# GpSimd's long operations and two VectorE steps put elsewhere in slots 3 to 13 of an attention and Fourier-layer kernel

## What is computed

```python
n1 = layernorm(x)
q, k, v = n1 @ wq + bq, ctx @ wk + bk, ctx @ wv + bv
s = (q @ k.T) / sqrt(32) * mask
s = where(s == 0, -1e9, s)
x = x + (softmax(s) @ v) @ wo + bo
n2 = layernorm(x)
out = x + real(ifft(fft(n2) @ (w_real + i * w_imag))) + bias
```

## Time and profile before

| what | value |
|---|---|
| median of 3 runs | 449.24 us (449.22 to 450.0) |
| the profiled execution | 449.74 us, its span 448.0 us |
| PE busy | 431.6 us, 96% of the span |
| DVE busy | 402.7 us, 90% |
| ACT busy | 368.2 us, 82% |
| POOL busy | 361.0 us, 81% |

### The profile page before, as it was taken

The page is one execution under the profiler, slowest core; times in us unless marked ns, Lnnn a source line. Parts: engine busy times, 40 slices in busy tenths (PEclk is TensorE's granted clock), DMA queues, the critical chain, the costliest instruction groups (busy, mean ns, idle before and its releaser), DMA issues.

```text
span 448.0 us, 10895 instructions
## 1 busy us (share of the span) xinstructions
PE 431.6 (96%) x3496; PEld 298.1 (67%) x3496; DVE 402.7 (90%) x532; ACT 368.2 (82%) x1342; POOL 361.0 (81%) x482
## 2 busy tenths in 40 slices
PE   7989999998899999999999999999999999989997
PEld 6877678786576666666776667666666765555444
DVE  3799899899999999999999999999999899999353
ACT  1648989799889989898989998989999899999620
POOL 5769997995779898989989898989898778755763
PEclk9999999999999999999999999999999999999999
DMA  8999754404434454545456554555442324431243
GB/s 271 397 385 221 249 190 113 129 1 119 113 105 93 136 126 119 148 117 139 128 139 137 129 145 113 121 104 130 137 95 64 97 75 96 78 83 35 61 115 121
DMA packets 85286, 60.15 MB, mean 134 GB/s; under 512 B 40141, under 2 KB 72813, under 8 KB 84718
## 3 DMA queue, kind: packets, MB, share of 16 engines
q1 hardware_dynamic: 84508, 59.29, 49.0%
q10 hardware_dynamic: 722, 0.17, 0.2%
HBM read 29.33 MB, written 8.39 MB: 84 GB/s over the span
## 4 chain that ended last, share of the span: by engine, by line
PE 68%; DVE 14%; issue 6%; ACT 5%; POOL 5%; DMA 1%; DVEq 0%; SPq 0%; POOLq 0%; ACTq 0%
PE bank L464 27%; PE bank L469 18%; PE bank L623 8%; PE bank L637 5%; DVE zs L924 4%; PE scores L609 4%; ACT zs L726 3%; DVE zs L917 3%; PE bank L570 2%; POOL cl L1164 2%; PE bank L551 1%; DVE nmin L929 1%; DMA cxs<-in_ctx 1%; PE scores L469 1%; DVE x L902 1%
## 5 line engine op out<-in xcount | busy, mean ns | idle before, releaser
L726 ACT ACTIVATE zs<-zs,nbias 128x128 f32<-128x128 f32 x512 | 199.5, 395 | 18.0 <-POOL nbias L1151 17.3
L726 ACT ACTIVATION_READ_ACCUMULATOR zs<-zs,nbias 128x1 f32 x512 | 98.4, 192 | 0.0
L924 DVE SCALAR_TENSOR_TENSOR zs<-zs 128x1024 f32<-128x1024 f32 x64 | 92.1, 1439 | 1.1
L929 DVE TENSOR_REDUCE nmin<-zs 128x8 f32<-128x1024 f32 x64 | 78.1, 1220 | 2.1
L917 DVE TENSOR_TENSOR zs<-scores,ms 128x1024 f32<-128x1024 f32 x64 | 78.0, 1219 | 0.1
L735 ACT COPY pt<-bank 128x512 f32<-128x512 f32 x128 | 67.8, 580 | 7.4 <-PE bank L623 7.3
L623 PE MATMUL bank<-ident,zs 128*128 128x128 f32 x512 | 67.0, 274 | 1.9 <-ACT zs L726 1.9
L1111 POOL TENSOR_TENSOR xs<-xs,bob 128x512 f32<-128x512 f32 (+1 forms) x41 | 42.8, 1048 | 24.7 <-DVE zs L924 21.6
L623 PEld LDWEIGHTS bank<-ident,zs 128*128 128x128 f32 x512 | 57.5, 140 | 5.6 <-ACT zs L726 4.5
L469 PE MATMUL bank<-xth,wqh 128*128 128x256 f16 x224 | 61.2, 273 | 0.0
L469 PE MATMUL bank<-xth,wql 128*128 128x256 f16 x224 | 61.1, 273 | 0.0
(11 more groups left out here) (125 smaller groups left out, 910.8 us busy)
## 6 DMA issues: line engine op xcount, KB each, us to landing
xs<-in_x SPq DMA_DIRECT2D x16, 512.0 KB, 4.7
xtr<-in_xt SPq DMA_DIRECT2D x16, 512.0 KB, 4.4
out<-x SPq DMA_DIRECT2D x31, 256.0 KB, 2.5
qs<-qh SPq DMA_DIRECT2D x120, 64.0 KB
lp<-in_lparts SPq DMA_DIRECT2D x4, 1024.0 KB, 9.9
qs<-ql SPq DMA_DIRECT2D x60, 64.0 KB
ms<-in_mask SPq DMA_DIRECT2D x16, 128.0 KB, 2.4
wks<-in_wk SPq DMA_DIRECT2D x2, 512.0 KB, 6.8
```

The lines of the kernel that those rows point to most:

```text
L726: last = act.activation(z, z, ACT.Exp, bias=nbias[:, s % 4, i:i + 1], scale=-NEG, accum_out=zsum[:, s % 4, i:i + 1])
L924: dve.scalar_tensor_tensor(out=z, in0=z, scalar=0.0, in1=z, op0=ALU.is_equal, op1=ALU.subtract).then_inc(eq_done, 1)
L929: dve.tensor_reduce(nmin[:, s % 4, :], zs[:, s % NZ].rearrange("p t h k -> p (t h) k"), AX.X, ALU.min).then_inc(mn_done, 1)
```

## The change

Nothing is computed differently, and the same DMAs are issued. Steps move to other places in the lists:

- POOL waits for the zero test of the slot (`eq_done`) from slot 4 on instead of slot 9 on. The long operations of slots 4 to 7 are put behind this wait: fold 6 (was in slot 3) before the bias of slot 4, folds 7 to 9 behind it; fold 10 before and fold 11 behind the bias of slot 5.
- `split_lo` of block 3 moves from slot 3 to slot 6, that of block 4 one slot later, from 6 to 7; each is cut into two halves, one before and one behind the slot's bias. `scale_mask(2)` moves from slot 4 to slot 6.
- `add_bo` of block 2 moves from slot 9 to slot 10; `add_bf(0, 0)` goes behind `scale_mask` in slot 12.
- DVE takes the moments of block 6 in slot 8 (were in slots 10 and 11) and puts them and the moments of the first output rows ahead of M(0)'s rows.
- SP loads `xtr` of block 5 behind the query copies of slot 5 instead of ahead of them.

```diff
--- before.py
+++ after.py
@@ -18,7 +18,6 @@
 NC = NB * S // CH
 NS = 4 * NC
 V0, V1 = 2, NS + 16
-VS = 9
 VP = 4
 VQ = 13
 LAST = ("FF", NC - 1, 1)
@@ -102,7 +101,7 @@
 
 
 def stats_slot(c, t):
-    return 4 if c == 4 else 4 * (c - 4) + 2 + t
+    return 4 if c == 4 else 8 if c == 6 else 4 * (c - 4) + 2 + t
 
 
 def small_slot(c):
@@ -113,13 +112,9 @@
     return 5 if c == 4 else 4 * (c - 3)
 
 
-def lo_slot(c):
-    return 3 if c == 3 else 6
-
-
 def bo_slot(c):
 
-    return c + 7 if c < 3 else 4 * c + 3 if c < 13 else 2 * c + 27
+    return c + 7 if c < 2 else 10 if c == 2 else 4 * c + 3 if c < 13 else 2 * c + 27
 
 
 def build(nc, x, xt, ctx_in, mask, wq, bq, wk, bk, wv, bv, wo, bo, lparts, tables, bf, eye, sums, pick, places, heads, out):
@@ -438,7 +433,9 @@
                     load_mask(c + 2)
                 if r == 0 and 0 <= c - 4 < NC:
                     store(c - 4, 1)
-                if r == 0 and 5 <= c + 4 < NC:
+                if v == 6:
+                    load_xt(5)
+                if r == 0 and 6 <= c + 4 < NC:
                     load_xt(c + 4)
                 if r == 3 and 0 <= c - 2 < NC - 1:
                     turn_x1n(c - 2, 0)
@@ -1054,7 +1051,7 @@
                 if 0 <= v - 9 < 4:
                     low_m(v - 9)
                 for n in mids:
-                    if fills[n][0] == "M":
+                    if fills[n][0] == "M" and v > 8:
                         lo(n)
                 tasks = []
                 tasks += [(stats1, mean1, a, t) for a in range(4, NC) for t in range(2) if stats_slot(a, t) == v]
@@ -1068,6 +1065,8 @@
                     recip((v - 3) // 2)
                 for _, mean, *ct in tasks:
                     mean(*ct)
+                if v == 8:
+                    lo(at["M", 0])
                 if c - 2 == NC - 1 and r < 2:
                     last_lo2(r)
                 if v == 2:
@@ -1230,8 +1229,6 @@
                 c, r = divmod(v, 4)
                 if v == 8:
                     constant_row()
-                if v == VP:
-                    fold(7)
                 for a in range(5, NC):
                     if small_slot(a) == v:
                         stat_cols(a)
@@ -1239,8 +1236,16 @@
                     rstd2(c - 2, 0)
                 if r == 2 and 0 <= c - 2 < NC:
                     rstd2(c - 2, 1)
-                if VS <= v < NS:
+                if VP <= v < NS:
                     pool.wait_ge(eq_done, v + 1)
+                if v == 4:
+                    fold(6)
+                if v == 5:
+                    fold(10)
+                if v == 6:
+                    split_lo(3, slice(0, 2), False)
+                if v == 7:
+                    split_lo(4, slice(0, 2), False)
                 for a in range(5, NC):
                     if v == 4 * a - 11:
                         split_lo(a, slice(0, 2), False)
@@ -1253,15 +1258,19 @@
                         add_bo(a, 1)
                 if 0 <= v < NS:
                     bias(v)
-                for n in {2: (4, 5), 4: (8, 9), 5: (10, 11)}.get(v, ()):
+                for n in {2: (4, 5), 4: (7, 8, 9), 5: (11,)}.get(v, ()):
                     fold(n)
+                if v == 6:
+                    split_lo(3, slice(2, 4))
+                if v == 7:
+                    split_lo(4, slice(2, 4))
                 if v % 2 == 1 and 0 <= v - 5 < NS:
                     ctx_lo((v - 5) // 2)
                 if r == 2 and 0 <= c - 2 < NC - 1:
                     norm_lo2(c - 2, 0)
                 if r == 3 and 0 <= c - 2 < NC - 1:
                     norm_lo2(c - 2, 1)
-                if r < 2 and 0 <= c - 3 < NC:
+                if r < 2 and 0 <= c - 3 < NC and v > 12:
                     add_bf(c - 3, r)
                 if v == 3:
                     low_o(0)
@@ -1279,15 +1288,14 @@
                         add_bo(a, 1, slice(0, D // 2), False)
                     if bo_slot(a) + 3 == v:
                         add_bo(a, 1, slice(D // 2, D))
-                for a in (3, 4):
-                    if lo_slot(a) == v:
-                        split_lo(a)
-                if v == 3:
-                    fold(6)
                 if v > VP and v % 2 == 1 and 0 <= v - 3 < NS:
                     spread((v - 3) // 2)
-                if r == 0 and 2 <= c + 1 < NC:
+                if v == 6:
+                    scale_mask(2)
+                if r == 0 and 3 <= c + 1 < NC:
                     scale_mask(c + 1)
+                if v == 12:
+                    add_bf(0, 0)
 
 
 def frequencies():
```

## The result

The changed kernel takes 456.6 us (median of 4 runs) against 449.36 us for the kernel before, measured again beside it: a ratio of 1.0167, 95% interval 1.015 to 1.0183, 7.2 us slower. The profiled execution took 456.56 us with a span of 454.8. The forecast was 455.4 us, range 451.7 to 457.8.

A forecast was written before the change was run, and what follows sets the result against it. PE was taken as the bound, its earlier losses paid in full at the end. Terms -4.3 + 7.3 + 0.6 + 2.6 = +6.2 us took the profiled 449.74 to 455.9, or 455.4 us against the 449.24 median; range 451.7 to 457.8.

The forecast's parts named there:

- `split_lo` of block 3, +7.3 us: PE idles before QQ(3, 0) from 62.8 us until `xtl` is complete at 70.1 us: +7.3 us, bounds 6.5 and 8.3.
- the stretch of the zero test of slot 6 by `rzb`: Within the block 3 term: zero test of slot 6 meets POOL's `rzb`, takes 1.6 us and ends at 67.5 us.
- +0.3 us: Zero test of slot 6, waiting for all of `rzb`, would end some 0.3 us later; sum 0.3 us higher, not adopted.
- `split_lo` of block 4, +0.6 us: PE waits before QQ(4, 0) for POOL's second half in slot 7: +0.6 us, 0 to 1.5.
- The clock, +2.6 us: PE's clock falls in the idle before QQ(3, 0), so matmuls after it run slowly: +2.6 us, between 0 and 2.6.
- The rival in which it stays up: Same stall before QQ(3, 0), but no slow matmuls after it: 452.8 us, chance 0.25.
- The waits that go, -4.3 us: PE's waits from 28 to 120 us, outside slot 1, all go: -4.3 us, -4.8 to -1.3.
- both long waits: PE's two waits of the scores for `mask_mul`, in slots 11 and 13, taken at 1.5 us each.
- The rival in which "`ml` and the others are not" guarded and POOL moves into them: DVE doesn't catch up; long waits of slots 11 and 13 stay, 3.0 us more: 458.4 us, chance 0.08.
- My sign "no wait over 1 us before the scores of slots 11 and 13": Sign in the profile after that the forecast is right: PE has no such wait in slots 11 and 13.
- The sum: Whole kernel: the four terms, -4.3, +7.3, +0.6 and +2.6 us, make +6.2 us.
- 4 us of freed DVE time: DVE up to slot 13: 0.8 + 0.65 + 0.54 + 1.25 + 1.0, about 4 us, set against long waits of 1.5 + 1.5 us.

The follow-up runs named there:

- experiment 1: Changed kernel with `split_lo` of block 3 whole and back at the end of slot 3, all else as changed: 448.46 us, ratio 0.9977.
- experiment 2: Kernel before with only `split_lo` of block 3 moved to slot 6 in halves, and SP's load of block 5 with it: 457.7 us, ratio 1.019.
- experiment 6: Changed kernel with `split_lo` of block 3 whole, right behind the bias of slot 4, its halves in slot 6 removed: 448.27 us, ratio 0.9978.
- experiment 7: As experiment 6, with the halves of `split_lo` of block 4 in slot 6 instead of slot 7: 448.17 us, ratio 0.9978.
- experiment 3: Changed kernel with 60 extra matmuls, their results overwritten, on PE in place of the wait before QQ(3, 0): 454.44 us, ratio 1.0106.
- experiment 4: Changed kernel with 30 extra matmuls, their results overwritten, on PE before QQ(3, 0): 456.01 us, ratio 1.0153.
- experiment 5: Changed kernel with the halves of `split_lo` of block 3 in slot 5, ahead of folds 10 and 11: 449.55 us, ratio 1.0013.
- experiment 8: As experiment 7, with `add_bo` of block 2 in slot 11 instead of slot 10: 451.37 us, ratio 1.0049.
- experiment 10: As experiment 7, with DVE's moments of block 6 and order around M(0) as before the change: 448.86 us, ratio 1.0001 to the kernel before.

## Why the prediction was right, and where it wasn't

**`split_lo` of block 3, +7.3 us.** Right: 7.1 us; undone alone (experiment 1) it gives back the whole loss, and done alone (experiment 2) it makes it. The step that I had from the earlier trace rows and that was off is the stretch of the zero test of slot 6 by `rzb`: it took 1.22 us, not 1.6, while `rzb` took 1.62 where 0.6 is its undisturbed length. In this case's rows it is the operation that started first that keeps its length: here the zero test at 65.19, ahead of `rzb` at 65.26. In slot 8 of the kernel before, from which I took the 1.6, the zero test had started behind POOL's additions for `xs` (78.13 to 80.63) and was held up by them, by 0.5 us; `rzb` at 80.59 then found the zero test already running, and waited for it in its turn, 1.0 us.

I had put the zero test's 0.54 us down to `rzb`, and took its part stretch as evidence against full waiting. The Trainium skill, SBUF — State Buffer, Who interferes with whom, has the shared ports as an exclusive lock: whoever holds it is waited for in full. Both slots agree with that, and so does `ml` at 107.40, 0.8 us too long beside an `x1nl` that had started at 107.18. What failed was my reading of who came first: with the zero test first, the rule gives nothing where I gave it +0.3 us (with `rzb` first it would have given +0.2: 0.6 us of waiting where I had 0.4). That the term came out all the same is luck: `xtl` stands behind `rzb` in POOL's list, and what the zero test didn't lose, `rzb` lost. The zero test ended at 66.41, 1.1 us earlier than I had it (0.6 of that is the lead from slot 1), and `xtl` began only at 66.85.

**`split_lo` of block 4, +0.6 us.** Right: a wait of 0.59 us at 85.32. Part of it (0.3 us) is there in experiment 6 as well, and taking it away changed no time that can be told (experiment 7).

**The clock, +2.6 us.** Right in kind, 2.2 to 2.3 us in size: 4.9 against 2.6 us for QQ(3, 0), and 456.6 against 454.44 us with the clock kept up (experiment 3). The rival in which it stays up falls; the granted clock of 0.50 is in the rows. The rule of the Trainium skill, TensorE: Matmul & The Clock Gate, Part 1, that idling brings the lower clock back, agrees with the trace: clock 1.00 to 0.50 in an idle time of 7.1 us. My price came from another place, the start, where the profile's clock column reads 1.00 and the slow matmuls are known by their length alone; no row had shown that a price read there holds for an idle time in mid-stream. It held to within 0.4 us.

**The waits that go, -4.3 us.** This step failed, in its size and in its reason. Some 2.6 us went. The step was: "PE comes into these slots over 5 us later than before, DVE only about 4", so that DVE catches up and both long waits vanish. It takes DVE's time up to slot 13 as one account. In the trace DVE had caught up long before: it stood still for 7.5, 2.1 and 0.3 us in slots 6 and 7 and for another 1.15 us in slot 8, each time for something that comes from PE. The wait of slot 11 is made behind that. From PE's first matmul of M(0) in slot 8 to the scores of slot 11 it is 19.54 us in the changed kernel (M(0) begins at 91.40, the scores at 110.94) and the same 19.54 in experiments 1, 3, 4, 5, 6, 7 and 8, with the stall, with a filled, a short or no stall, and 1.2 us of wait are in it each time. Time won ahead of slot 8 doesn't reach that wait.

Behind slot 8 the parts work against each other. The DVE part shortens the wait of slot 11 by 0.8 us, and the POOL part lengthens it by 0.6 us; the traces put that down to `ml` of slot 10, 0.8 us longer; that the wait of slot 13 went is the work of both, and more of the POOL part (the table under experiment 10). I had counted POOL's moves as relief alone. The rival in which "`ml` and the others are not" guarded and POOL moves into them, to which I gave 0.08, came half true: one of its two long waits stayed. Which of POOL's moves brings `x1nl` ahead of `ml`, and what part of slot 13 is `add_bf` going behind `scale_mask`, wasn't tested apart; the one try at that neighbourhood (experiment 8) didn't shorten `ml`. My sign "no wait over 1 us before the scores of slots 11 and 13" holds for slot 13 and not for slot 11 (1.18).

The sum was 6.2 and the measured 7.2 us: -0.2 on the stall, -0.3 on the clock, +1.7 on the old waits make 7.4, and 0.2 stay unexplained, which is inside the interval. The one term that was mis-sized by more than 0.5 us is the gain.

**DVE's time in the sum.** I let 4 us of freed DVE time pay for 3 us of waits. Experiments 1 and 6 show how little of it reaches PE: 1.7 us in slot 4 are 0.2 us at most, because that slot's DVE is released by PE and ACT (`us` waited 0.81 us for `od`) and not by its own queue. What reached PE in these runs is what lies behind DVE's idle time in slot 8.

## What to carry to other kernels

Before a step is moved back on one engine, find on every other engine the first instruction that asks for it, and in whose list it stands ahead of what; here one f16 remainder, three slots later on the least critical engine, stopped PE for 7 us and took its clock for another 2. A stall of the bound engine doesn't cure its later waits: look for the last place where the lagging engine itself waits for the bound one (here slot 8), since a lag that hurts later is made behind that place, and only work moved there counts. When one part of a change shortens a wait and another part lengthens it, only the parts run alone show it. Relief for an engine is worth looking for only in the slots where the bound engine waits for it by name.

## What the runs showed of the hardware

The clock went down in an idle time of 7.1 us, and in one of 3.7 us as well (experiment 4), and stayed up in those of 1.9 us in the traces (experiment 5, and slot 1 of the kernels before and after). Some other executions of experiment 5, three of ten, had a mean clock of 0.996, and so had two of twelve of experiment 10, so it isn't shown that 1.9 us always leave it up. On top of the idle time itself, 8.5 us of it cost 2.5 us, 7.1 us 2.3, and 3.7 us 1.4.

Of a DVE operation with two inputs in SBUF and a POOL operation that overlap, the one that starts second is stretched, by about what is left of the first: `rzb` takes 1.62 instead of 0.6 us behind a zero test that keeps its 1.22, and `ml` 1.49 instead of 0.68 behind an `x1nl` that keeps its 1.17. The zero test had started only 0.07 us ahead of `rzb`; experiments 1, 3 and 4 show the same pair 0.08 to 0.10 us apart, with `rzb` at 1.60 or 1.61 us. The opposite order at so small a distance doesn't occur in these traces.
